# Two attention constants in a two-block kernel: FP32 products at the end of the first row group, or three-term products in the third group

## The reference

```python
xn = _layernorm(x, axis=-1)
s = _L0_attn_ref(xn, ...)            # a linear map of xn, RMS norm, plus xn
g = _silu(_L0_ffn_ref(xn, ...))      # W2 . fwht(silu(W1 x) * (W3 x)), 256 -> 1024 -> 256
x = x + s * g
xn = _layernorm(x, axis=-1)
s = _L1_attn_ref(xn, qkv, o_proj, gamma, beta)   # causal attention over 256-wide q, k, v
g = _silu(_L1_ffn_ref(xn, ...))
x = x + s * g
```

## Time and profile before

| | |
|---|---|
| median of 3 runs | 355.83 us (355.63 to 355.95) |
| the profiled execution: its own time | 355.57 us |
| its span in the profile | 353.8 us |
| TensorE busy | 348.7 us, 99% |
| VectorE, ScalarE, GpSimd busy | 252.5, 168.3, 106.3 us |
| granted TensorE clock | full in all slices |

### The profile page before, as it was taken

One profiled execution on the slowest core, in us unless ns is written; L12 is line 12 of the kernel. 1 busy time (PEld: TensorE's weight loads), 2 busy tenths in 40 slices (PEclk: granted clock), 3 DMA queues, 4 the chain that ended last, 5 costly groups with the idle time before them and its releaser, 6 DMA issues.

```text
span 353.8 us, 4943 instructions
## 1 busy us (share of the span) xinstructions
PE 348.7 (99%) x1761; PEld 295.9 (84%) x1761; DVE 252.5 (71%) x498; ACT 168.3 (48%) x332; POOL 106.3 (30%) x122
## 2 busy tenths in 40 slices
PE   8999999999999999999999999999999999999996
PEld 5888888888888888888978878888888888888896
DVE  5679964995499666966588876788657886467645
ACT  2865442447254713454465644654346544464510
POOL 2164410466126943663025030150300703004000
PEclk9999999999999999999999999999999999999999
DMA  7989769205160403130342401626014251054001
GB/s 239 255 184 225 150 111 130 74 26 138 41 143 13 120 0 119 31 122 0 104 138 51 127 2 59 179 45 196 3 56 144 70 159 50 1 191 134 3 0 61
DMA packets 69648, 34.44 MB, mean 97 GB/s; under 512 B 40692, under 2 KB 69624, under 8 KB 69624
## 3 DMA queue, kind: packets, MB, share of 16 engines
q1 hardware_dynamic: 69480, 34.06, 38.0%
q10 hardware_dynamic: 144, 0.07, 0.1%
HBM read 21.99 MB, written 12.12 MB: 96 GB/s over the span
## 4 chain that ended last, share of the span: by engine, by line
PE 94%; ACT 2%; DVE 2%; DMA 1%; SPq 0%; issue 0%; ACTq 0%
PE GU L358 20%; PE GU L359 20%; PE GU L360 20%; PE O L358 8%; PE O L359 8%; PE O L360 8%; DMA stage<-in_L_ffn_W 1%; PE O L426 1%; PE O L509 1%; PE O L508 1%; PE O L507 1%; PE T L365 1%; PE T L360 1%; PE T L358 1%; PE T L359 1%; ACT PZ L809 1%
## 5 line engine op out<-in xcount | busy, mean ns | idle before, releaser
L722 ACT ACTIVATE hf<-GU 128x512 f32<-128x512 f32 x64 | 38.2, 599 | 80.4 <-DVE hid L841 64.3
L997 DVE TENSOR_TENSOR hf<-hf,GU 128x512 f32<-128x512 f32 x64 | 43.5, 680 | 28.4 <-PE GU L360 22.6
L358 PE MATMUL GU<-XT,W1T 128*128 128x512 f32 x128 | 50.6, 396 | 0.1
L841 DVE TENSOR_TENSOR hid<-hf,hid 128x512 fp32r<-128x512 f32 x64 | 50.5, 791 | 0.3
L360 PE MATMUL GU<-XT,W1T 128*128 128x512 f32 x128 | 49.9, 390 | 0.0
L359 PE MATMUL GU<-XT,W1T 128*128 128x512 f32 x128 | 49.9, 390 | 0.0
L358 PE MATMUL GU<-XT,W3T 128*128 128x512 f32 x128 | 49.9, 389 | 0.0
L360 PE MATMUL GU<-XT,W3T 128*128 128x512 f32 x128 | 49.8, 389 | 0.0
L359 PE MATMUL GU<-XT,W3T 128*128 128x512 f32 x128 | 49.8, 389 | 0.0
L358 PE MATMUL O<-hid,W2hi 128*128 128x512 f32 x112 | 44.0, 393 | 0.0
L359 PE MATMUL O<-hid,W2hi 128*128 128x512 f32 x112 | 43.7, 390 | 0.0
(11 more groups left out here) (204 smaller groups left out, 724.9 us busy)
## 6 DMA issues: line engine op xcount, KB each, us to landing
swap_rows<-GX SPq DMA_DIRECT2D x7, 512.0 KB, 3.3
sT<-swap_rows SPq DMA_DIRECT2D x28, 128.0 KB, 2.7
swap_gate<-GX SPq DMA_DIRECT2D x7, 512.0 KB, 2.9
sT<-swap_gate SPq DMA_DIRECT2D x28, 128.0 KB, 2.7
stage<-in_L_ffn_W SPq DMA_DIRECT2D x12, 256.0 KB, 4.3
swap_p<-PX SPq DMA_DIRECT2D x4, 640.0 KB, 3.4
PL<-swap_p SPq DMA_DIRECT2D x16, 160.0 KB, 3.1
stage<-in_L_ffn_W SPq DMA_DIRECT2D x32, 64.0 KB, 2.7
```

Of the source, the lines that this page charges most:

```text
L358: pe.matmul(o, lhs(0), rhs(0), start=start, stop=False)
L722: act.activation(hf[:, c % 2, :], GU[:, c % 2, 0, :], ACT.Silu).then_inc(silu_done, 1)
L841: dve.tensor_tensor(dst, src, hi_part.bitcast(F32), ALU.subtract).then_inc(done, 1)
L997: dve.tensor_tensor(hf[:, c % 2, :], hf[:, c % 2, :], GU[:, c % 2, 1, :], ALU.mult).then_inc(mul_done, 1)
```

## The change

`small_av` moves from the end of the head into the third group, behind its up chunk 0, and becomes three-term. Its operands are split beforehand: ScalarE rounds the three parts of wqkvT and wo into `avH` behind chunk 6 of the second group (four instructions), and POOL makes the four residues `avL` between `nat_lo` and the second `pair_lo` of the second group. `turn_wqkv` moves on VectorE from the head to behind chunk 5 of the second group, ahead of `x_turn`. The results' rounding on ScalarE and `small_lo(1)`, `small_lo(2)` on VectorE go to behind chunk 2 of the third group, on VectorE ahead of the gate product. The Hadamard product of pair 5 and its `pair_u` go from behind chunks 1 and 2 to behind chunks 3 and 4. The wait on `sm_lo` 3 goes there as well. `wqkvT` and `wo` now lie where AR and VR will be, and `avH`, `avL` where block 1's W1 and W3 will be.

```diff
--- before.py
+++ after.py
@@ -68,6 +68,9 @@
 
         X = sb("X", [P, NB * TILES, D])
         MR = sb("MR", [P, 2, KC, D], F32R)
+        with ExitStack() as early:
+            wqkvT = sb("wqkvT", [P, 3, KC, D], F32, early)
+            wo = sb("wo", [P, KC, D], F32, early)
         AR = sb("AR", [P, 2, KC, D], F32R)
         VR = sb("VR", [P, 2, KC, D], F32R)
         ident = sb("ident", [P, P])
@@ -112,12 +115,13 @@
         with ExitStack() as early:
             win = sb("win", [P, MC, D], F32, early)
             woutT = sb("woutT", [P, MC, D], F32, early)
-            wo = sb("wo", [P, KC, D], F32, early)
-            wqkvT = sb("wqkvT", [P, 3, KC, D], F32, early)
             ssm = sb("ssm", [P, 5, MC, DS], F32, early)
             kprod = sb("kprod", [P, 2, MC, DS], F32, early)
             kvec = sb("kvec", [P, MC], F32, early)
             gbrow = sb("gbrow", [2 * KC, P], F32, early)
+        with ExitStack() as early:
+            avH = sb("avH", [P, 2 * TILES, KC, D], F32R, early)
+            avL = sb("avL", [P, 2 * TILES, KC, D], F32R, early)
         W1T = (W1T0, sb("W1T1", [P, 2, KC, H], F32R))
         W3T = (W3T0, sb("W3T1", [P, 2, KC, H], F32R))
         U, U2, W2hi, W2lo = [], [], [], []
@@ -186,6 +190,7 @@
         w_turned, wx_hi, wx_lo, natx_hi, natx_ready = sem("w_turned"), sem("wx_hi"), sem("wx_lo"), sem("natx_hi"), sem("natx_ready")
         kv_loaded = sem("kv_loaded")
         wout_loaded, wqkv_loaded, wo_loaded = sem("wout_loaded"), sem("wqkv_loaded"), sem("wo_loaded")
+        av_hi, av_lo = sem("av_hi"), sem("av_lo")
         wout_turned, wqkv_turned, win_scaled = sem("wout_turned"), sem("wqkv_turned"), sem("win_scaled")
         xnext_loaded = sem("xnext_loaded")
         w2_loaded, w2_turned = sem("w2_loaded"), sem("w2_turned")
@@ -429,18 +434,18 @@
 
             def small_av():
 
-                pe.wait_ge(wqkv_turned, 3)
-                pe.wait_ge(wo_loaded, 16)
-                for i in range(KC):
-                    for c in range(KC):
-                        last = pe.matmul(T[:, 0, i * D:(i + 1) * D], wqkvT[:, 0, c, i * P:(i + 1) * P], wqkvT[:, 1, c, :],
-                                         start=(c == 0), stop=(c == KC - 1))
-                last.then_inc(sm_mm, 1)
-                for i in range(KC):
-                    for c in range(KC):
-                        last = pe.matmul(T[:, 1, i * D:(i + 1) * D], wqkvT[:, 2, c, i * P:(i + 1) * P], wo[:, c, :],
-                                         start=(c == 0), stop=(c == KC - 1))
-                last.then_inc(sm_mm, 1)
+                pe.wait_ge(av_lo, 4)
+                pe.wait_ge(u_ready, PAIRS + 1)
+
+                def part(w):
+
+                    return lambda a, c: (avH, avL)[a][:, 2 * w + 1, c, :]
+
+                for q, (left, right) in enumerate(((part(0), part(1)), (part(2), part(3)))):
+                    for i in range(KC):
+                        for c in range(KC):
+                            last = mm3(T[:, q, i * D:(i + 1) * D], lambda a: left(a, c)[:, i * P:(i + 1) * P], lambda a: right(a, c), c == 0, c == KC - 1)
+                    last.then_inc(sm_mm, 1)
 
             def first_x_transposes():
 
@@ -550,10 +555,8 @@
                 up_chunk(0, 0, 6, True)
                 small_m()
                 up_chunk(0, 0, 7, True)
-                small_av()
                 pe.wait_ge(sm_lo, 1)
                 recurrent_mix(0)
-                pe.wait_ge(sm_lo, 3)
 
             def block0_group(n):
                 if n == 1:
@@ -562,7 +565,11 @@
                     down_chunk(0, n - 1, i)
                 for c in range(HC):
                     up_chunk(0, n, c, False)
-                    if c == 1 and n > 1:
+                    if c == 0 and n == 2:
+                        small_av()
+                    if c == (3 if n == 2 else 1) and n > 1:
+                        if n == 2:
+                            pe.wait_ge(sm_lo, 3)
                         next_hadamard(PAIRS + 2 * n - 3)
                 if n < 3:
                     next_hadamard(PAIRS + 2 * n - 2)
@@ -763,7 +770,6 @@
                 w2_hi(0)
                 chunk(0, 7, True)
                 hid_hi_chunk(0, 7)
-                small_hi([(flat[1], T[:, 0, :]), (flat[2], T[:, 1, :])], 2, sm_mm, 2, sm_hi)
 
             def block0_group(n):
                 act.wait_ge(hid_ready, 8 * n)
@@ -773,7 +779,13 @@
                 act.wait_ge(ssq_ready, 4 * n)
                 for c in range(HC):
                     chunk(n, c, False)
-                    if c == 2 and n > 1:
+                    if c == 6 and n == 1:
+                        for w in range(3):
+                            hi(avH[:, 2 * w + 1, :, :], wqkvT[:, w, :, :], wqkv_turned, w + 1, av_hi)
+                        hi(avH[:, 7, :, :], wo[:, :, :], wo_loaded, 16, av_hi)
+                    if c == 2 and n == 2:
+                        small_hi([(R[:, 0, :, :].rearrange("p k d -> p (k d)"), T[:, q, :]) for q, R in enumerate((AR, VR))], 2, sm_mm, 2, sm_hi)
+                    if c == (4 if n == 2 else 2) and n > 1:
                         pair_u(1, PAIRS + 2 * n - 3, 2 * n - 3)
                     if c == 3 and n < 3:
                         turned_hi(PAIRS + 2 * n - 2)
@@ -1016,6 +1028,11 @@
 
             def between_chunks(n, c, last=False):
 
+                if c == 5 and n == 1:
+                    turn_wqkv()
+                if c == 2 and n == 2:
+                    small_lo(1)
+                    small_lo(2)
                 if c == (2 if n < NB else 1):
                     gate_product(n - 1)
                 if n < 3:
@@ -1097,7 +1114,6 @@
                 chunk(0, 5)
                 x_turn(1)
                 chunk(0, 6)
-                turn_wqkv()
                 w2_sums(0)
                 small_lo(0)
                 w2_lo(0, 0)
@@ -1105,8 +1121,6 @@
                 w2_lo(0, 1)
                 dve.wait_ge(xrest_loaded, 16)
                 dve.wait_ge(small_loaded, 16 * N_SMALL)
-                small_lo(1)
-                small_lo(2)
                 hid_lo_chunk(0, HC - 1)
 
             def block0_group(n):
@@ -1259,6 +1273,12 @@
                 pool.wait_ge(natx_hi, j + 1)
                 pool.tensor_tensor(w2nat[:, 1, :, :], U2[1][:, 2 * j:2 * j + 2, :], w2nat[:, 0, :, :].bitcast(F32), ALU.subtract).then_inc(natx_ready, 1)
 
+            def av_residues():
+
+                for w, src in enumerate((wqkvT[:, 0, :, :], wqkvT[:, 1, :, :], wqkvT[:, 2, :, :], wo[:, :, :])):
+                    pool.wait_ge(av_hi, w + 1)
+                    pool.tensor_tensor(avL[:, 2 * w + 1, :, :], src, avH[:, 2 * w + 1, :, :].bitcast(F32), ALU.subtract).then_inc(av_lo, 1)
+
             def rms_of(n):
                 pool.wait_ge(ssq_ready, 4 * n + 4)
                 pool.tensor_tensor(rtmp[:, :], ssq[:, :], rms_eps[:, :], ALU.add).then_inc(rms_step, 1)
@@ -1301,6 +1321,8 @@
                 if n > 1:
                     pair_butterfly(1, 2 * n - 3, PAIRS + 2 * n - 2)
                     quad_butterfly(1, n - 2, (17, 23)[n - 2])
+                if n == 1:
+                    av_residues()
                 if n < 3:
                     pair_lo(PAIRS + 2 * n - 1)
                 else:
```

## The result

| | before | changed |
|---|---|---|
| median of 22 runs | 355.85 us | 356.30 us |
| lowest, highest | 355.46, 356.40 | 356.04, 357.34 |
| profiled execution, its span | 355.57, 353.8 us | 356.49, 354.7 us |

The ratio is 1.0016, 95% interval 1.0009 to 1.0022; in the medians the changed kernel is 0.45 us longer (356.30 / 355.85 = 1.0013). The forecast was 355.95 (355.0 to 357.0) and no change of over 0.2%. The time lies in that range and the ratio within the 0.2%, its upper end just above. But the interval excludes a ratio of 1, so the changed kernel is a little slower, and it excludes the forecast's own ratio too, 355.95 / 355.83 = 1.0003.

What follows compares the result with a forecast made beforehand. TensorE's work, busy 348.7 of 353.8 us, plus its waits was taken as the bound. -3.59 + 2.85 + 0.76 + 0.1 = +0.12 on 355.57 gave 355.69; with the median 0.26 higher, 355.95 us, range 355.0 to 357.0.

Steps and rivals of the forecast that it cites:

- Work taken away, -3.59: End of the head: removing small_av's F32 products and its wait from TensorE saves 3.59 us.
- added, +2.85: Third group: 24 matmuls of 256 columns, as many as in a mix, add 2.85 us on TensorE.
- The wait at the mix of the head, +0.76: Head's mix waits for MR's residue on VectorE, behind sums held up by POOL's butterfly: +0.76 us.
- Rival A: Head: sums go first or share with POOL, so the 0.76 goes; 355.5 us, or 355.1; chance 0.20.
- The second group, 0 us: Second group: transposes and POOL's residues delay VectorE, but mix, third down chunk and x_lo cost TensorE 0 us.
- the gate, +0.1: Gate's scatter through DRAM falls among U2's loads and may delay VectorE, hence TensorE: +0.1 us, range to 1.4.
- Rival C: Gate comes 1.4 us late on VectorE and this reaches the second group's mix: 357.2 us; chance 0.06.
- Rival B: Second group: POOL's four residues delay VectorE's last hidden residues, TensorE waits 0.95 at third down chunk: 356.9 us; chance 0.13.
- The third group, 0 us: Third group: VectorE's later products and the Hadamard product at 116.33 cost TensorE 0 to 0.1, taken as 0.

Runs made afterwards that it cites:

- e5: Changed kernel with the two constants at their new place as plain F32 products, without ScalarE's roundings and POOL's four residues: 356.92 us, ratio 1.0038 to the kernel before.
- e9: Changed kernel with POOL's last butterfly of the head held until VectorE's W2 sums are done: 356.15 us, ratio 1.0006 to the kernel before.
- e1: Changed kernel with MR's residue put ahead of the W2 sums on VectorE in the head: 355.74 us, ratio 0.9997 to the kernel before.
- e6: Changed kernel with small_av ahead of the third group's chunk 0 and the results' rounding and residues behind chunk 1: 355.98 us, ratio 1.0007 to the kernel before.

## Why the prediction was right, and where it was off

The time fell in the range and the main mechanism was the forecast one. The forecast's middle was 0.35 us too low, outside what the interval allows.

*Work taken away, -3.59, and added, +2.85.* Both held. The constants took 2.87, and e5 put the difference to F32 at 0.59 in the trace, with times that agree.

*The wait at the mix of the head, +0.76.* Right in mechanism and place: the mix started at 41.67, forecast 41.57, the sums held up by POOL until 41.02, forecast 40.92. e9 showed the exclusion and e1 the price, 0.56 in the medians. With chunk 7 as early as in the one trace I had, the wait is 0.71 (e5). It is smaller where chunk 7 comes later than VectorE and POOL do: by 0.25 in the changed kernel's profile, from the transposes of W2 on, which leaves 0.49. Rival A is refuted: the rows of two exclusions and POOL's head start were enough to decide it.

*The second group, 0 us, and the gate, +0.1.* The product of chunk 6 was forecast to come at the very moment it is wanted; it did, and cost the tenth that a short wait costs, 0.3 where the gate was late. That tenth stands where the forecast had its 0.1 for the gate, so the term's size was right for another reason: luck. The lateness of the scatter was forecast at 0 to 2 us and was 1.0 once, 0.45 once and 0 five times; the small value was the right one. Rival C is a tail, not the rule. The hidden residues and `x_lo` did not reach TensorE; the last residue ended at 83.23, 0.4 us ahead of the third down chunk. Rival B is refuted by this trace, and e5 says the same: without POOL's residues nothing is gained there. (Of the two rows called for it, the first lost 1.39 - 0.65 = 0.74 and not 0.8; nothing hangs on it.)

*The third group, 0 us.* This is the step that failed inside a forecast that came out right. I looked for the nearest wait among VectorE's products and the late Hadamard product at the group's end ("against an old slack of 0.85 and more at each product", "the closest is the Hadamard product at 116.33"), and passed over the wait that the change itself puts there: the moved Hadamard product waits for `sm_lo` 3, VR's residue. From the trace its end could have been worked out: VectorE's product of chunk 2 ends 0.95 behind TensorE's start of chunk 3, then come three residues of 0.6, 2.75 us in all, against a chunk of 2.72, and the semaphore on top. It cost 0.2 in each trace of a kernel that has it, and e6, without it, was 0.2 to 0.3 faster.

*Restarts.* Nowhere in the sum stood the tenth that TensorE loses behind each wait. The third group's is in its 0.2 and the second mix's stands for the gate's 0.1; the head's is another 0.1. The missed 0.2 and this tenth are 0.3 of the 0.35 us between 355.95 and 356.30. What is left is less than the medians resolve.

## What to carry to other kernels

Taking work out of an engine's queue ahead of a critical instruction buys nothing if what stands between them waits for another engine's instruction at a shared resource (here 1.9 us of transposes were taken out and the sums grew by 1.8): move the critical instruction ahead of the one that will be held up, which here cost nothing and gave the most. Of a change that moves work into a group, first cost the waits that the change itself writes down, with the queue behind them, before looking at the old ones. On a kernel whose one engine is 99% busy, each short wait costs its length and a tenth more.

## What the runs showed of the hardware

- Two instructions with two SBUF operands each, one on VectorE, one on POOL, wait for each other whole: 1.21 us against 3.40 for the same sums. A residue on VectorE with one operand in PSUM isn't held: 0.69 in the midst of POOL's butterfly (39.11 in e9, the butterfly 38.97 to 41.37). When VectorE's residue ended at 37.70 in the changed kernel, POOL's butterfly, entered at 37.23, went ahead of VectorE's sums, entered at 37.62; whether the first to stand goes first or the two take turns, these rows don't tell.
- Behind a short wait of TensorE the second matmul of 512 columns follows at 0.33 instead of 0.23 us (105.70 to 106.03 in the changed kernel, 47.07 to 47.41 in e9), one of 256 columns at 0.23 instead of 0.12 (41.67 to 41.90 in the changed kernel).
- The first three-term matmul of 512 columns behind F32 products is followed at 0.42 instead of 0.23 us (97.44 to 97.86 in e5; the same in the head, behind MR's product).
- In F32, a product of 256 columns costs 3.46/8 = 0.43 us, the slow step behind the last one included; as three rounded ones it costs 2.87/8 = 0.36. The third term's splitting was hidden on the other engines here.
- The granted clock was 0.998 of full or above in every profile, so none of this is the clock's.
